# Cross-attention over a long memory: keys, mask, residual and result on eight DMA engines, values on twelve

## The reference

```python
mu = jnp.mean(hidden_states, axis=-1, keepdims=True)
var = jnp.var(hidden_states, axis=-1, keepdims=True)
x = (hidden_states - mu) * jax.lax.rsqrt(var + LN_EPS) * ln_gamma + ln_beta
Q = _split_heads(x @ Wq.T)
K = _split_heads(memory_keys)
V = _split_heads(memory_values)
scores = jnp.einsum('bhsd,bhtd->bhst', Q, K) * HEAD_DIM ** (-0.5)
scores = jnp.where(attention_mask[:, None, None, :], scores, -jnp.inf)
probs = jax.nn.softmax(scores, axis=-1)
attn = jnp.einsum('bhst,bhtd->bhsd', probs, V)
out = attn.transpose(0, 2, 1, 3).reshape(B, S, HIDDEN) @ Wout.T
return residual + out
```

## Time and profile before

| | |
|---|---|
| runs shown | 1488.03, 1495.26, 1503.92 us |
| median | 1495.26 us |
| the profiled execution's time | 1497.4 us |
| its span, first to last instruction | 1495.6 us |
| its mean granted TensorE clock | 0.963 of full speed |
| PE busy | 1352.0 us, 90% |
| DVE busy | 1088.4 us, 73% |
| ACT busy | 769.7 us, 51% |
| POOL busy | 388.8 us, 26% |
| DMA | 226.37 MB, mean 151 GB/s |

### The profile page before, as it was taken

The page is one execution under the profiler, slowest core; times in us unless marked ns, Lnnn a source line. Parts: engine busy times, 40 slices in busy tenths (PEclk is TensorE's granted clock), DMA queues, the critical chain, the costliest instruction groups (busy, mean ns, idle before and its releaser), DMA issues.

```text
span 1495.6 us, 88664 instructions
## 1 busy us (share of the span) xinstructions
PE 1352.0 (90%) x40736; PEld 1037.6 (69%) x40736; DVE 1088.4 (73%) x3452; ACT 769.7 (51%) x847; POOL 388.8 (26%) x371
## 2 busy tenths in 40 slices
PE   6999989999999989999999989989998998889986
PEld 4347777777667777777777767767776777677775
DVE  6657778788777777877777877878786777777640
ACT  2126555555555555555455555555554554555463
POOL 1011323332322233322222332322223222223221
PEclk8999999999999999999999999999999999999899
DMA  8314555555545544555555554555555444454430
GB/s 271 99 38 150 163 160 160 161 159 159 166 152 162 166 156 154 161 163 158 156 158 173 162 161 150 167 153 161 170 166 153 145 151 158 147 170 145 131 98 21
DMA packets 126358, 226.37 MB, mean 151 GB/s; under 512 B 11619, under 2 KB 71555, under 8 KB 125987
## 3 DMA queue, kind: packets, MB, share of 16 engines
q1 hardware_dynamic: 125986, 220.71, 47.7%
HBM read 216.90 MB, written 3.77 MB: 148 GB/s over the span
## 4 chain that ended last, share of the span: by engine, by line
PE 66%; DVE 26%; issue 6%; ACT 2%; DMA 0%; POOL 0%; SPq 0%; POOLq 0%; DVEq 0%; ACTq 0%
DVE masked L347 22%; PE ps L325 22%; PE ps L268 21%; PE ps L309 12%; PE ps L284 5%; PE ps L707 4%; PE ps L301 2%; DVE den_inv L383 2%; ACT probs L391 1%; PE ps L275 1%; DVE tile_max L347 1%; DMA v<-in_wq_t 0%; DVE probs L612 0%; PE ps L698 0%; DVE den L376 0%
## 5 line engine op out<-in xcount | busy, mean ns | idle before, releaser
L347 DVE CUSTOM_DVE_ANT_0 masked<-ps,mask_tile 112x500 bf16<-112x500 f32 x1536 | 974.1, 674 | 327.4 <-PE ps L268 315.1
L391 ACT ACTIVATE probs<-ps,mask_bias 125x1344 f32<-125x1344 f32 x384 | 530.6, 1382 | 629.6 <-PE ps L309 629.6
L268 PE MATMUL ps<-kT,qdb 32*112 32x500 bf16 x1536 | 496.6, 423 | 45.5 <-DVE tile_max L347 35.8
L309 PE MATMUL ps<-qd,kT 32*125 32x112 f32 x12288 | 478.7, 277 | 13.6 <-issue 13.4
L309 PEld LDWEIGHTS ps<-qd,kT 32*125 32x125 f32 x12288 | 475.1, 190 | 21.7 <-issue 18.0
L325 PE MATMUL ps<-probs,v 125*32 125x56 f32 x24576 | 410.4, 218 | 38.0 <-issue 36.1
L325 PEld LDWEIGHTS ps<-probs,v 125*32 125x32 f32 x24576 | 343.7, 113 | 132.7 <-issue 125.5
L268 PEld LDWEIGHTS ps<-kT,qdb 32*112 32x112 bf16 x1536 | 156.3, 125 | 208.2 <-DVE tile_max L347 158.9
L393 ACT ACTIVATE probs<-ps,mask_bias 125x448 f32<-125x448 f32 x384 | 240.7, 627 | 0.0
L435 POOL COPY v<-v_stage 125x2048 f32<-125x2048 f32 x96 | 181.7, 1892 | 201.1 <-DMA v_stage<-in_ctx 201.1
L301 PE MATMUL ps<-max_rows,ones_row 4*125 4x448 bf16 x1536 | 213.7, 391 | 7.9 <-ACT probs L391 5.5
(11 more groups left out here) (48 smaller groups left out, 295.6 us busy)
## 6 DMA issues: line engine op xcount, KB each, us to landing
kT<-in_kt SPq DMA_DIRECT2D x384, 250.0 KB, 3.1
v_stage<-in_ctx SPq DMA_DIRECT2D x384, 250.0 KB
mask_tile<-mask_add SPq DMA_DIRECT2D x96, 109.4 KB, 4.5
x_res<-in_x SPq DMA_DIRECT2D x16, 224.0 KB, 5.6
out<-result SPq DMA_DIRECT2D x16, 224.0 KB, 5.4
probs<-in_x SPq DMA_DIRECT2D x14, 224.0 KB, 8.4
v<-in_wq_t SPq DMA_DIRECT2D x1, 1024.0 KB, 6.0
woutT<-in_wout_t SPq DMA_DIRECT2D x1, 1024.0 KB, 16.9
```

The source lines that it names most:

```text
L268: nc.tensor.matmul(bank[0:PAIR_Q, 0:KEYS], qdb[rows, b % 2, g, :], keys, start=True, stop=True).then_inc(ring_filled, 1)
L309: mm = nc.tensor.matmul(ps[0:LANES, score_bank(SLOTS * b + k, r), PAIR_Q * g:PAIR_Q * (g + 1)], kT[rows, b % 2, k // CHUNK, g, k % CHUNK, ...
L347: nc.vector.tensor_tensor_reduce(out=sums, in0=bank[0:PAIR_Q, 0:KEYS], in1=mask_tile[0:PAIR_Q, b % 2, KEYS * c:KEYS * (c + 1)], scale=1.0, ...
L391: nc.scalar.activation(probs[0:LANES, k % PROBS, 0:HELD_ROWS], ps[0:LANES, 0:HELD_ROWS, 0:BANK_Q], ACT.Exp, bias=bias, scale=SCALE).then_i ...
```

## The change

Keys: the source in memory is laid out anew by the host, as [16, 8, ...], and load_k reads it as 8 groups of 16 rows. Values: the 125 rows are split into 120, read as 12 groups of 10, and 5 more in a transfer of their own, so that each quarter of a chunk is two transfers and v_landed counts twice as far; since the twelve groups are interleaved, keys and masks are put in the same order of lanes by the host (LANE_OF). Mask, residual and result: one side of each transfer is written as 8 groups of 14 rows. The store of the result moves from slot 4 to slot 5 and the load of the residual from slot 4 to slot 6. The bytes moved and the work of PE, DVE, ACT and POOL stay as they are.

```diff
+KEY_RINGS = 8
+VALUE_RINGS = 12
+ROW_RINGS = 8
+EVEN_LANES = LANES // VALUE_RINGS * VALUE_RINGS
+LANE_OF = [m for a in range(VALUE_RINGS) for m in range(a, EVEN_LANES, VALUE_RINGS)] + list(range(EVEN_LANES, LANES))
...
         def load_k(sp, b, c, g):
-            sp.dma_start(kT[:, b % 2, c, g].rearrange("p k m -> p (k m)"), kt[b, c, :, KEYS * g:KEYS * (g + 1)]
-                         ).then_inc(k_landed[b % 2][c], 16)
+            sp.dma_start(kT[:, b % 2, c, g].rearrange("p k m -> p (k m)"), kt[b, c, :, :, KEYS * g:KEYS * (g + 1)].rearrange("j a n -> a j n")).then_inc(k_landed[b % 2][c], 16)
...
-            src = ctx[b, KEYS * c:KEYS * (c + 1), :].rearrange("(m k) n -> m k n", k=CHUNK)
+            src = ctx[b, KEYS * c:KEYS * (c + 1), :].rearrange("(m k) n -> m k n", k=CHUNK)[:, k]
+            even = src[0:EVEN_LANES].rearrange("(j a) n -> a j n", a=VALUE_RINGS)
...
-            sp.dma_start(v_stage[0:LANES, n % STAGES, k], src[:, k]).then_inc(v_landed[n % STAGES], 16)
+            sp.dma_start(v_stage[0:EVEN_LANES, n % STAGES, k], even).then_inc(v_landed[n % STAGES], 16)
+            sp.dma_start(v_stage[EVEN_LANES:LANES, n % STAGES, k], src[EVEN_LANES:LANES]
+                         ).then_inc(v_landed[n % STAGES], 16)
...
-            sp.dma_start(mask_tile[0:PAIR_Q, b % 2, keys], mask_add[b:b + 1, keys].broadcast_to([PAIR_Q, KEYS])
+            sp.dma_start(mask_tile[0:PAIR_Q, b % 2, keys], 
+                         mask_add[b:b + 1, keys].unsqueeze(1).broadcast_to([ROW_RINGS, PAIR_Q // ROW_RINGS, KEYS])
...
-            sp.dma_start(x_res[0:PAIR_Q, :], x_rows[d]).then_inc(res_landed, 16)
+            sp.dma_start(x_res[0:PAIR_Q, :], x_rows[d].rearrange("(a j) n -> a j n", a=ROW_RINGS)).then_inc(res_landed, 16)
...
-            sp.dma_start(out_rows[d], result[0:PAIR_Q, :]).then_inc(result_stored, 16)
+            sp.dma_start(out_rows[d].rearrange("(a j) n -> a j n", a=ROW_RINGS), result[0:PAIR_Q, :]).then_inc(result_stored, 16)
...
-            pool.wait_ge(v_landed[n % STAGES], 16 * CHUNK * (n // STAGES + 1))
+            pool.wait_ge(v_landed[n % STAGES], 2 * 16 * CHUNK * (n // STAGES + 1))
...
-                    if k == CHUNK and b % 2 == 0 and b > 0:
-                        if b > 2:
-                            store_result(sp, b // 2 - 2)
+                    if k == CHUNK + 1 and b % 2 == 0 and b > 2:
+                        store_result(sp, b // 2 - 2)
+                    if k == CHUNK + 2 and b % 2 == 0 and b > 0:
                         load_residual(sp, b // 2 - 1)
...
-    keys = ctx.reshape(BATCH, CHUNKS, LANES, CHUNK, BLOCKS, 128)
-    lanes = mask.reshape(BATCH, CHUNKS, LANES, CHUNK)
+    keys = ctx.reshape(BATCH, CHUNKS, LANES, CHUNK, BLOCKS, 128)[:, :, LANE_OF]
+    lanes = mask.reshape(BATCH, CHUNKS, LANES, CHUNK)[:, :, LANE_OF]
+    key_rows = keys.transpose(0, 1, 5, 4, 3, 2).reshape(BATCH, CHUNKS, KEY_RINGS, 128 // KEY_RINGS, BLOCKS * KEYS)
```

More of the change, by code:

```diff
@@ L762 @@
     mask = np.ascontiguousarray(inputs["mask_BxS2_bf1"]).view(np.uint8)
-    keys = ctx.reshape(BATCH, CHUNKS, LANES, CHUNK, BLOCKS, 128)
-    lanes = mask.reshape(BATCH, CHUNKS, LANES, CHUNK)
+    keys = ctx.reshape(BATCH, CHUNKS, LANES, CHUNK, BLOCKS, 128)[:, :, LANE_OF]
+    lanes = mask.reshape(BATCH, CHUNKS, LANES, CHUNK)[:, :, LANE_OF]
+    key_rows = keys.transpose(0, 1, 5, 4, 3, 2).reshape(BATCH, CHUNKS, KEY_RINGS, 128 // KEY_RINGS, BLOCKS * KEYS)
     host = {
         "x": np.ascontiguousarray(inputs["x"]),
-        "kt": np.ascontiguousarray(keys.transpose(0, 1, 5, 4, 3, 2)).reshape(BATCH, CHUNKS, 128, BLOCKS * KEYS),
+        "kt": np.ascontiguousarray(key_rows.transpose(0, 1, 3, 2, 4)),
         "ctx": ctx,
```

## The result

| | before | changed |
|---|---|---|
| median | 1497.78 us (4 runs) | 1580.97 us (1563.78 to 1588.92, 4 runs) |
| ratio | | 1.052, 95% interval 1.041 to 1.063 |
| profiled execution | 1497.4 us | 1580.75 us |
| span, granted clock | 1495.6 us, 0.963 | 1578.9 us, 0.941 |

The change makes the kernel 5% slower, where 4% faster was forecast.

A forecast was written before the change was run, and what follows sets the result against it. It took PE to bound the kernel, with 49.5 us of late-fetch stalls plus 27 us of clock. Terms -66 (loop), +2 (start), +1 (end), -2 (other stalls) gave -65: 1497.4 to 1432 us, range 1408 to 1470.

The forecast's parts named there:

- one engine for all fetches: PE's instruction fetches: all sit on one DMA engine, one of the eleven that carry no values.
- the case of the forecast: Main loop: fetch on an engine without data, batches 41.1 us in place of 43.30, 1432 us; chance 0.68.
- Rival C: Main loop: fetch on an engine with keys and newly values; 320 fetches lose 125 us, 1622 us; chance 0.12.
- rival B: Main loop: fetch on one of four engines keeping values; 50 us gained, 1448 us; chance 0.12.
- Four have no data in the loop: Main loop: with keys, mask, residual and result on eight engines, four engines carry no data.
- the term for the end: After the loop: last residual and result move 14 rows per engine in place of 7, costing 1.3 us.
- If all issue stalls go: Main loop: a batch is then at the floor, 40.7 us; 41.1 was taken, gaining 66 us over 30 batches.
- The start: Ahead of the loop: batch 0's keys on eight engines delay the mask rows' store, 0 to 8.5 us; 2 taken.
- one transfer at 0.43: SP's issuing in the loop: values in two transfers add 12 DMAs a batch, 5 us of SP's 41; cost 0.
- Slots of their own: Main loop, result and residual at k 5 and 6: worth something only where their engines still serve the fetch, otherwise 0.
- Issue waits above 50 us: PE's issue waits: a sign that the forecast is wrong and the fetch's engine now carries keys and values.
- A share of q8 below 1.5%: Instruction-fetch queue q8: a sign that the forecast is right, as an undisturbed fetch is shorter.

The follow-up runs named there:

- no keys in the loop: The kernel before without the 360 key loads of the loop, later batches computing with the keys of batches 0 and 1: 1466.02 us, ratio 0.980.
- the slots alone: The kernel before with one edit, store of the result at slot 5 and load of the residual at slot 6: 1478.15 us, ratio 0.985.
- values on six: The kernel before with store and residual at slots 5 and 6, and values in 6 groups of 20 rows and 5 apart: 1535.49 us, ratio 1.027.
- the value pairs: The kernel before with store and residual at slots 5 and 6, and value quarters loaded in pairs in odd slots: 1577.53 us, ratio 1.052.

## Where the prediction went wrong

**Right:** that the issue waits are instruction fetches, and that data transfers make them late (the block edges; no keys in the loop); that a long stall costs clock as well, 27 us in all before the change (the slots alone took back 24.8); the number of engines that the shapes of keys, masks and values give. That none of the five value engines serves fetches fits values on six against five, but the value pairs leave a doubt.

**The step that failed: one engine for all fetches.** The prediction says "It is on one of the other eleven", from a single fetch at 338.1 us, and then speaks of "its engine" and splits the outcomes by where that one engine lies. That fetch was one of a round of eight. With eight engines in the round, and none among the five, freeing some and loading others is certain, and the case of the forecast, a fetch engine without data, comes near for three of eight fetches. Rival C is what the two hot positions show: about 50 us of stalls in place of some 9; rival B is the three between. None of the three was the answer; the answer was all of them at once, and the hot ones decide: they have 49.7 of the 92.5 us of stalls. That rival C had the sign right is luck in part: it has one engine, 320 late fetches and 1622 us.

**"Four have no data in the loop" was not so.** The prediction has mask, residual and result on eight engines. The masks went there; the residual and the result did not (the 4-byte packets), so a burst on all sixteen engines was left, on the quiet four too. That also makes the term for the end, 1.3 us for 14 rows per engine, empty: what stands behind the last copy grew by 0.7 us.

**The gain of the quiet positions was sized wrong too.** "If all issue stalls go" took the whole 49.5 us for data's doing. The three quiet positions still have 12.6 us of stalls, 4.2 each. The six positions other than 1 and 5 had 26.1 us before the change, 4.4 each. So apart from the store and the residual in one slot there was next to nothing to take away, and much to add; that burst was the only part of the 66 us that was there to be had, and the slots alone took it. The delays say the same: before the change a fetch started on average 1.36 us after its block was entered; in the quiet positions it is 1.07 to 1.29 us.

**The start** was put at 2 us, bounds 0 to 8.5; it was 17.5. The chain of the first 130 us has SP's own issuing in it (start us, us, what); behind it the store of the mask rows on SP's timeline, before and after, and the windows up to the first copy, before and after:

```profile
18.34 1.99 SPq L227
20.38 1.46 SPq L227
...
28.83 9.73 DMA mask_add<-rows_add
39.99 5.60 DMA mask_tile<-mask_add
...
18.55 0.73 SPq L492 DMA_DIRECT2D mask_add<-rows_add  x1
...
28.83 1.21 SPq L500 DMA_DIRECT2D mask_add<-rows_add  x1
...
0.00:146.80 146.80, 129.24 (x1579) 73.14 (x1583) 94.81 (x278) 48.41 (x74) 20.23 (x31) 0.94 0.45 139
...
0.00:164.30 164.30, 138.21 (x1577) 77.74 (x1581) 94.47 (x278) 48.40 (x73) 20.19 (x31) 0.89 0.41 123
```

A price left out is that of issuing. All issues of a key quarter, before, and then of the changed kernel's three transfers (ns, least, median, most):

```profile
L222 SPq DMA_DIRECT2D kT<-in_kt x384: 346/347/3377, 5.1 to 1415.7; - x192
```

```profile
L227 SPq DMA_DIRECT2D kT<-in_kt x384: 588/627/2359, 5.2 to 1494.2; - x192
...
L238 SPq DMA_DIRECT2D v_stage<-in_ctx x384: 779/786/1488, 42.7 to 1537.9; - x192
...
L239 SPq DMA_DIRECT2D v_stage<-in_ctx x384: 451/460/636, 43.6 to 1538.8; - x192
```

A key transfer takes SP 0.63 us in place of 0.35, and the values 0.79 + 0.46 us, where the prediction added one transfer at 0.43. That is 1.87 us a slot, and 0.68 more in a slot with a mask. In the loop SP's waiting covers it. At the start nothing does: the mask rows' store stands behind 12 key transfers, and SP reaches it 10.3 us later than before. 12 x 0.28 us of issuing are 3.4 of these; the rest is issues that took longer still (up to 1.99 us), for a reason that no run gives. The store itself lands as fast as before (9.73 us, before 10.3). DVE, which needs the masks, takes its first tile at 46.19 us in place of 37.15. And the wait costs clock here too: up to the first copy it is 0.89 in place of 0.94, and PE is busy for 9.0 us longer over nearly the same instructions. So the 17.5 us are about half idle time, near the bound of 8.5 us that was made of packets only, and half clock, which had no term.

**Slots of their own** were valued at nothing where the fetch's engine is free. By themselves they were the one part that paid, 1.5%. The burst was read rightly in the earlier trace rows, and its gain then given to the wrong edit.

**What stays open.** The 65 us in the loop are placed (stalls 30, clock 27, waits for DVE 8), and two hot positions hold over half of the stalls. Why 12 more key transfers a batch, or value transfers in pairs, delay fetches in most positions is not known. That the fetches go round eight engines is read from positions; the trace doesn't name the engine of a packet.

**The signs.** Issue waits above 50 us were the sign of rival C, and they came (57.1 and 23.4 us in the two lines). A share of q8 below 1.5% was a sign of the forecast and came too (1.4%), only because the span is longer: a fetch takes 1.12 us on average, before 1.13.

## What to carry to other kernels

Long straight-line PE code is itself a stream of transfers (here 320 of 16 KB). Look for idle stretches at a fixed instruction count, number the fetches, and sort their delays by number before deciding which DMA engines to keep free; one fetch seen on one engine says nothing of the next. Spreading bursts in time (a store and a load in slots of their own) was safe and worth 1.5%; narrowing transfers to fewer engines made some fetches wait far longer than it helped the others. Check the number of engines of every changed transfer by its 4-byte packets: two of five here had not moved. When a transfer's shape changes, price its issue on SP as well as its packets, above all where SP isn't waiting for anyone.

## What the runs showed of the hardware that was not expected

- The stalls behind PE's instruction fetches have the pattern of a round over eight of the sixteen DMA engines in a fixed order, starting at another place in different kernels' traces: two neighbours hot at 6 and 7, at 3 and 4, at 1 and 2 (28.7 and 21.0, 24.8 and 17.5, 28.6 and 20.0 us of stalls).
- Issuing a transfer whose rows were put in 8 or 12 groups took SP 0.63 and 0.79 us, a plain one 0.35 us. Where the groups of 14 rows lie one behind the other in memory (residual, result) the edit changed nothing: sixteen engines, 0.34 us for a store.
- Two value quarters at once, on the five engines of the values, cost 8% against the slots alone (1606 against 1478 us), while twice as many value transfers, of half the size and spread as before, cost nothing (1482 us). In the first a fetch took 1.31 us on average in place of 1.13.
- With stalls of up to 1.6 us the clock over the loop stayed at 1.00 (slots alone); with stalls of up to 1.8 us it read 0.98 (no keys in the loop) and with up to 2.7 us 0.97 (before). Between 0.97 and 1.00 lie 24.8 us of PE's busy time.
